# When POOL may begin its next group of gathers: two groups before the one that the sums have reached, in place of four

## The reference, cut to what matters

```
msg = h[src]                                   # gather a row per edge
out = segment_sum(msg, dst, num_segments=N)    # add the rows of one destination
```

## Time and profile before

| | |
|---|---|
| median of 3 runs | 12801.77 us (12754.38 to 12835.04) |
| the profiled execution's own time | 12898.33 us |
| its span, first to last instruction | 12895.1 us |
| PE, DVE, POOL busy | 4042.5, 3867.4, 8187.2 us |
| mean granted TensorE clock | 0.592 of full speed |
| pass 0, 1, 2, 3, 4 (first gather to last) | 2403, 2692, 2406, 2721, 2426 us |

### The profile page before, as it was taken

One profiled execution on the slowest core, in us unless ns is written; L12 is line 12 of the kernel. 1 busy time (PEld: TensorE's weight loads), 2 busy tenths in 40 slices (PEclk: granted clock), 3 DMA queues, 4 the chain that ended last, 5 costly groups with the idle time before them and its releaser, 6 DMA issues.

```text
span 12895.1 us, 84333 instructions
## 1 busy us (share of the span) xinstructions
PE 4042.5 (31%) x18630; PEld 3047.8 (24%) x18631; DVE 3867.4 (30%) x4123; ACT 472.8 (4%) x740; POOL 8187.2 (63%) x8343
## 2 busy tenths in 40 slices
PE   1332333243343344222222224444444432222222
PEld 1111111122222222111111113433343321111111
DVE  3323323333333333344344312222222221111111
ACT  0000000011111111000000000000000000000000
POOL 4666666666666666677667665555565556666666
PEclk7565556566666666555555556676676665555555
DMA  4333333344344444213333212222222221111111
GB/s 91 99 96 92 98 92 98 90 133 120 114 129 129 122 131 122 60 34 56 56 55 62 43 40 62 62 62 60 61 64 63 61 44 37 36 36 36 36 36 35
DMA packets 712143, 951.29 MB, mean 74 GB/s; under 512 B 289361, under 2 KB 504401, under 8 KB 709597
## 3 DMA queue, kind: packets, MB, share of 16 engines
q0 software_dynamic: 266240, 385.62, 14.7%
q10 hardware_dynamic: 208528, 441.95, 11.4%
q1 hardware_dynamic: 237075, 120.64, 3.2%
HBM read 737.19 MB, written 206.15 MB: 73 GB/s over the span
## 4 chain that ended last, share of the span: by engine, by line
another core or an unknown queue 36%; issue 28%; PE 12%; POOL 9%; DVE 8%; DVEq 3%; ACT 2%; ACTq 1%; DMA 1%; SPq 0%; POOLq 0%
POOL flat L282 9%; PE pair L1068 5%; PE pair L918 3%; DVE flat L418 2%; PE wide L932 1%; PE flip L989 1%; DVEq L214 1%; PE flip L990 1%; DVE flat L680 1%; DVEq L418 1%; ACT flat L814 1%; DVE flat L522 1%; ACT flat L810 1%; DVE flat L575 1%
## 5 line engine op out<-in xcount | busy, mean ns | idle before, releaser
L282 POOL DMA_INDIRECT flat<-table,stage x8320 | 8182.5, 983 | 4687.4 <-issue 2447.4
L918 PE MATMUL pair<-flat 128*128 x9760 | 1582.9, 338 | 5305.8 <-issue 3750.8
L918 PEld LDWEIGHTS pair<-flat 128*128 x9760 | 1185.0, 132 | 5767.1 <-issue 5700.5
L1068 PE MATMUL pair<-flat 128*128 x4880 | 1190.7, 412 | 1535.4 <-DVE flat L680 1234.5
L418 DVE TENSOR_TENSOR flat<-fixed,dcol 128x1024 f32 x915 | 1076.9, 1218 | 1901.3 <-remote 1133.8
L1068 PEld LDWEIGHTS pair<-flat 128*128 128x128 f32 x4880 | 1076.7, 248 | 1649.5 <-issue 1648.3
L680 DVE TENSOR_TENSOR flat<-fixed,dcol 128x512 f32<-128x512 f32 x610 | 417.4, 690 | 1809.7 <-remote 1298.7
L460 DVE TENSOR_REDUCE batch<-pair 128x65 f32<-128x195 f32 (+1 forms) x392 | 139.4, 356 | 2627.9 <-remote 1524.2
L932 PE MATMUL wide<-flat,wbd 128*128 128x512 f32 x840 | 594.7, 860 | 351.6 <-DMA flat<-gate_d 137.3
L989 PE MATMUL flip<-ident,flat 128*128 128x128 f32 x840 | 352.5, 422 | 989.7 <-ACT flat L814 480.0
L418 DVE TENSOR_TENSOR flat<-fixed,flat 128x1024 f32 x305 | 362.1, 1220 | 931.5 <-remote 589.6
(11 more groups left out here) (142 smaller groups left out, 1811.6 us busy)
## 6 DMA issues: line engine op xcount, KB each, us to landing
flat<-table,stage POOLq DMA_INDIRECT x8320
flat<-in_ea ACTq DMA_DIRECT2D x140, 768.0 KB
ex_d<-flat ACTq DMA_DIRECT2D x140, 768.0 KB
flat<-ex_d SPq DMA_DIRECT2D x208, 512.0 KB
flat<-gate_d ACTq DMA_DIRECT2D x280, 192.0 KB
pm_d<-flat ACTq DMA_DIRECT2D x70, 768.0 KB
flat<-pm_d ACTq DMA_DIRECT2D x70, 768.0 KB
sort_d<-flat ACTq DMA_DIRECT2D x14, 1024.0 KB
```

What stands on the lines that cost most here:

```text
L282: pool.indirect_dma_start(out=to_row, out_offset=None, in_=tables[p], in_offset=bass.IndirectOffsetOnAxis(ap=stage[:, st, c:c + 1].bitcast ...
L918: mm = M(bank[a % 2][:, 0:width], flat[:, ds(at_one[k], P * 2)].bitcast(bf16), flat[:, ds(at_row[k], TW * 2)].bitcast(bf16)[:, 0:width], s ...
L1068: mm = M(bank[a % 2][:, 0:F3], ohf[:, k, :], exr[:, ds(g % XR, 1), k, :].rearrange("p o c -> p (o c)"), start=first and k == 0, stop=False)
```

## The change

One number in POOL's wait. Before, group g may begin when PE (DVE in pass 3) has increased `slots_free` to g - 3. After, it must be g - 1. The ring keeps its four slots and its addresses; the same gathers are issued in the same order.

```diff
 SLOTS = 4
+
+AHEAD = 2
 SG = 8
...
                     if g % SG == 0:
                         pool.wait_ge(staged[st], 16 * (p * (G // SG // 2) + g // SG // 2 + 1))
-                    if g >= SLOTS:
-                        pool.wait_ge(s["slots_free"], g - SLOTS + 1)
+                    if g >= AHEAD:
+                        pool.wait_ge(s["slots_free"], g - AHEAD + 1)
                     for k in range(CH):
```

## The result

The changed kernel takes 14342.8 us (median of 4 runs, 14308.03 to 14349.51) against 12805.31 us (4 runs, 12754.38 to 12835.04) of the kernel before on the same chip: ratio 1.1196, 95% interval 1.1165 to 1.1227. It is 12% slower. The forecast was 14,060 us: 1260 us were expected on top of the kernel before, and by the medians 1537 us came. The spans of the two profiled executions, 12895.1 and 14305.7 us, are only 1410.6 us apart, mostly because the profiled execution before took 93 us more than its median.

What follows compares the result with a forecast made beforehand. The prediction took POOL's issuing of gathers to bound the kernel, so POOL must not wait. Its terms, 560 + 310 + 390 + 0 = 1260 us on a median of 12802, gave about 14,060 us; range 13,250 to 16,100 us.

Steps and rivals of the forecast that it cites:

- Term 1: Passes 0, 2 and 4: gather, landing and PE form a loop, 12.5 us a group instead of 10.0; +560 us.
- the sign of being right: Profile after: windows of passes 0, 2 and 4 at 2600 to 2800 us would confirm the forecast.
- Term 2: Batch ends of passes 0, 2 and 4: PE returns 8 or 9 us beyond the group's 12.5 us; +310 us.
- Term 3: Pass 1: each further new group of a tile waits for PE, 14.0 us on top per tile; +390 us.
- Term 4: Pass 3: DVE frees the slots, PE and DVE set the pace, two groups ahead suffice; 0, up to +50 us.
- A: Rival: PE's increments stay late, 14.4 to 15.5 us a group in passes 0, 2, 4; 15,760 to 16,440 us; chance 0.22.
- B: Rival: gathering one group runs beside use of the other, so the time stays at 12,800 us; chance 0.07.
- C: Rival: pass 3 gains up to 640 us as POOL's pauses free PE's increments; 12,630 us, 1.3% faster; chance 0.06.

Runs made afterwards that it cites:

- three ahead: The kernel before, with POOL allowed to begin group g once PE has begun group g - 2: 11013.18 us, ratio 1.0065; repeated on another chip, 11020.9 us, ratio 1.0072.
- The experiment with the seventh matmul: The change, with PE telling POOL at its seventh matmul of a new group, not its first: 15139.37 us, 783.5 us more than the change beside it.
- first set: Follow-up kernels run on one chip without late increments, where the kernel before took 10941.02 us.
- third set: Follow-up kernels run on one chip without late increments, where the kernel before took 10943.55 us.
- the kernel with small loads: The change, with the forward scan's loads in pass 0 cut to two columns from the third step on: 13641.62 us (one run).

## Why the prediction was right, and where its terms were off

**What bounds the kernel.** Right that POOL must not wait, and it came out of the page and POOL's waits. A chip without late increments shows it best: with three ahead POOL is busy 8173.2 us, and the 0.30 us between gathers add 2509.7: 10,683 of a span of 11,012.2 us.

**Term 1, the plain group.** Right in kind: 2.24 + 0.62 = 2.86 us of wait in a plain group, forecast 2.8, and the median wait is 2.8 us in each of the four passes. The mean is 3.7 us over the 824 waits (3040.6 us). The fit of the Trainium skill that I had weighed against the row ("DMA: Bandwidth & Descriptors", Anatomy of one DMA: by it 2.1 us before SP can be told) was counted from the end of the gather and would so give 0.6 us more; the trace shows 2.24 us for landing, SP and PE together and disagrees with that use of it. Counted from the gather's start the two are near each other: 0.94 us of gather and 1.24 us to the last packet are 2.2 us. The experiment with the seventh matmul shows that the loop through PE is closed in every group. This term is mis-sized, because I took pass 4's rows for three passes; pass 0 ended outside the 2600 to 2800 us that I had named as the sign of being right. Pass 4 lasts 2623.5 us (floor forecast 2600). Pass 2 lasts 144.6 us more: 92.2 us of POOL busy (1661.94 for 1569.75), which stood already in the earlier trace rows, and 52.5 us of longer waits:

```profile
POOL flat L284 <- PE pair L920: 659.7, 206, 10.4
...
POOL flat L284 <- PE pair L920: 607.2, 206, 6.8
```

(pass 2, then pass 4). Pass 0 lasts 256.6 us more than pass 4: 16.7 busy, 239.9 in the waits (847.1 us, 4.1 each). With the scan's loads cut, pass 0 is 157.1 us shorter, so most of it is landing delayed by other transfers. Four slots had hidden that, and I priced the landing by the pass with the fewest transfers.

**Term 2, the batch ends.** Wrong in size, 310 us forecast. In pass 4 they cost about 2623.5 - 2600 = 24 us in place of 100. DVE starts 4.0 us after POOL's stop, where I had put 5 or 6; the step that failed is the one behind it. From DVE's reduction to PE's return it takes 6.2 us (12611.55 to 12617.72, and before the change too, 11348.53 to 11354.70 in the earlier trace rows). So by my own rows PE was due back some 12 us after POOL's stop, and not 20, which is less than the next group needs to be gathered. What is left is 3.9 us at each of 6 batch ends and nothing at the others. The errors of terms 1 and 2 have opposite signs: for the three passes 870 was forecast and 1035.9 came.

**Term 3, pass 1.** 390 forecast, 415.1 measured. That the number fits is luck, in two ways. The values of the working (19 to 22.4 us of work and 14.0 on top) add up to 33 to 36.4 us a tile and not 32 to 35, which would have made some 480 us. And the mechanism was another. POOL's waits for PE in pass 1:

```profile
POOL flat L284 <- PE pair L920: 926.6, 206, 21.9
```

That is 319.4 us more than in pass 4, and POOL's gathers take 164.2 us more (1733.95 for 1569.75, a price that the earlier trace rows show and that the term left out): together 483.6 us, all by which pass 1 is longer than pass 4 (3107.0 - 2623.5). So this pass too is the loop of gathering and waiting, its median wait is the 2.8 us of the others, and what makes its mean longer is mainly the landing, 2.2 us from a group's last gather to its last packet in place of 1.24. PE's transposes and DVE's scan, on which I had built the term, are on the path at few groups: PE begins over 1.5 us after the landing at 11 of 207.

**Term 4, pass 3.** 0 forecast, -19.1 measured, and 2730.7 us where only this pass has two ahead of three. It holds only because PE's late increments slow DVE there anyway (1310.3 us of waits, 1295.6 before), which I had seen for the kernel before but hadn't made a condition of the term; on this kind of chip that is luck: without them pass 3 takes 2104.4 us with three ahead and 2165.5 with two, so the same edit then costs 61 us.

**The cause.** That the loop through landing and PE sets the time after the change is shown: a signal that is 0.97 us later costs each group 0.93 us, landing alone costs most of it, and one group more of lead takes the cost away on either kind of chip.

I had also used that late increments come some microseconds after POOL's stop and hardly ever while it goes on. The first half stands, the second doesn't. The trace records each increment by itself. After the change the one of the matmul that ends at 12484.735 is recorded at 12484.748. Before it, those of the matmuls that end at 11200.497 and 11210.517 are recorded at 11223.505 and 11223.623, 5.5 us after POOL's last gather. So the increment itself is held, and POOL is not slow to take it up. I call an increment late if it is recorded over 1 us after any matmul that could have made it. Then 404 of 558 recorded in pass 4 before the change are late; 210 of them come after POOL has stopped, in the median 5.5 us after its last gather, but 172 come while POOL has been issuing for over 2 us. Unbroken issuing is not enough to make them late either: on other chips (three ahead, first set) 1 of 4066 is late in all passes. Why the chips differ stays open. The granted clock of pass 4 is 0.51 to 0.52 on both, and one run of three ahead in the third set, recorded with a granted clock of 1.0 in place of 0.62, took 11048.69 us for 11008.04 to 11029.34, so PE's clock doesn't make the two times. I found nothing in the records but the lateness itself that tells the chips apart; no trace of the kernel before was taken on a chip without it.

**The rivals.** A (increments stay late) is out: 0.62 us, no remote wait of POOL. B (hidden) is out: 824 waits. The practice of the Trainium skill that I put beside it ("Trainium Kernel Development and Optimization", Best Practices: double-buffer, so that DMA runs beside compute), read as I did, that two groups will do, disagrees with the trace; with three ahead (ratio 0.998 to 1.007) the landing runs beside the next group's gathers. C is out: pass 3 did not move.

**The size of the loss** depends on the chip, which the prediction could not see. The loop gives nearly the same passes on both kinds, so the ratio is 1.12 where the kernel before already pays for late increments. Where it doesn't, the kernel with small loads plus the 157 us that these save gives 13,800 us as an estimate, 1.26 of 10,941; the change itself wasn't run there.

## What to carry to other kernels

Count how many groups lie between the one that the producer wants to begin and the last one that the consumer must have reached: if the permission for a group comes from the consumer's start on the group issued just before it, landing and both signals are on the path of every group, however fast the consumer is. Here one group more (three ahead) hid nearly all of it; a fourth gave 0.7% on one kind of chip, and eight nothing on the other. When a lead that hid something is taken away, price what it hid for each pass by itself, with the transfers that run beside it there. And before a ratio is explained, see whether the kernel before takes the same time on another chip.

## What was unexpected of the hardware

The same kernel takes 10,941 us on some chips and 12,875 on others (12874.98 / 10941.02 = 1.177), on each chip within some 1%. The difference that the traces show is one: where POOL issues indirect gathers without a break, increments made by PE's matmuls are held. In the kernel before they reached POOL up to 24 us late and DVE 34 us (the tile's last matmul is over at 11314.4, DVE starts at 11348.53), and with eight slots PE's lag grew to 41 us on average. About half of the late ones come after POOL has stopped, mostly 4 to 6 us after its last gather in passes 0, 2 and 4, and in the order of the matmuls: six of them are recorded within 0.27 us, from 11223.471 to 11223.742. Of DVE's 2546 recorded increments in the same trace none is late by the same measure, and PE still starts 2.2 us after a group's last gather, so SP's sign isn't late there either.

POOL stopping for 2.8 us and more after each group removed nearly all of the lateness in the four passes where PE frees the slots: 62 late increments are left there, 52 of them in pass 1, where 1582 were. In pass 3, where POOL's stops are as before, 407 are left of 405. Pauses of 2.3 us every 20 us in pass 4 still leave 326 of 540 late, but the time lost to them falls from 340 to 71 us on top of what the pauses cost. A doubled ring removed nothing.
